# Border of the shared and routed expert stages: awaiting the output stores later, turning the first rows ahead of the register loads, and moving expert 0's last weight piece

## The reference

```python
h = rmsnorm(x, ln2_w)
t = h.reshape(-1, d)                       # T = 2048 tokens, d = 512
logits = t @ gate_w.T
probs = jax.nn.softmax(logits, axis=-1)
topv, topi = jax.lax.top_k(probs, K)       # K = 6 of E = 16 experts
topv = topv / jnp.sum(topv, axis=-1, keepdims=True)
cw = jnp.zeros((T, E), t.dtype).at[jnp.arange(T)[:, None], topi].add(topv)
g = jnp.einsum('td,eid->eti', t, eg_w)     # I = 352
u = jnp.einsum('td,eid->eti', t, eu_w)
hh = jax.nn.silu(g) * u
routed = jnp.einsum('eti,edi,te->td', hh, ed_w, cw)
shared = jax.nn.silu(t @ sg_w.T) * (t @ su_w.T) @ sd_w.T    # 704 = 2 x 352
out = x + (routed + shared).reshape(b, s, d)
```

## Time and profile before

| what | us |
|---|---|
| three runs: median | 2296.87 |
| three runs: lowest, highest | 2296.24, 2299.54 |
| the profiled execution's own time | 2293.54 |
| its span in the profile | 2291.5 |
| PE busy | 2163.1 (94% of the span) |
| DVE busy | 1180.4 (52%) |
| POOL busy | 989.1 (43%) |
| ACT busy | 690.7 (30%) |

### The profile page before, as it was taken

How to read it: one execution, slowest core, us unless ns; L and a number is a source line. 1 busy time by engine, 2 the same in 40 slices (tenths; PEclk the granted TensorE clock), 3 DMA queues, 4 the chain that set the end, 5 groups by cost and what they waited for, 6 DMA issues and landing times. The chain is left out here.

```text
span 2291.5 us, 40185 instructions
## 1 busy us (share of the span) xinstructions
PE 2163.1 (94%) x12066; PEld 1883.5 (82%) x12067; DVE 1180.4 (52%) x2533; ACT 690.7 (30%) x1609; POOL 989.1 (43%) x1043
## 2 busy tenths in 40 slices
PE   6879999999999999999994999979999999999997
PEld 4668888888888898888883767779999999998996
DVE  5736646564655646465665476533433333333342
ACT  5623334343333334333333211112222222222221
POOL 1225454553545454553546024424444444444443
PEclk9989999999999999999997999989999999999998
DMA  3113343343434344343336210076676676667443
GB/s 138 56 46 119 119 160 125 133 170 109 151 119 141 119 151 151 110 169 116 141 124 245 86 65 28 37 248 156 156 228 157 156 200 183 156 174 199 90 81 55
DMA packets 143417, 307.59 MB, mean 134 GB/s; under 512 B 17104, under 2 KB 17104, under 8 KB 141072
## 3 DMA queue, kind: packets, MB, share of 16 engines
q1 hardware_dynamic: 118128, 248.33, 30.9%
q0 software_dynamic: 24960, 58.21, 13.4%
q10 hardware_dynamic: 288, 0.53, 0.1%
HBM read 180.91 MB, written 126.09 MB: 134 GB/s over the span
## 5 line engine op out<-in xcount | busy, mean ns | idle before, releaser
L544 POOL TENSOR_TENSOR chunk_hi<-chunk_raw,zero 128x512 fp32r<-128x512 f32 x160 | 166.5, 1041 | 251.6 <-DMA chunk_raw<-in_whole 251.6
L1518 DVE TENSOR_TENSOR prod<-ps,silu 128x352 f32<-128x352 f32 x111 | 58.3, 525 | 313.4 <-PE ps L62 313.4
L546 POOL TENSOR_TENSOR chunk_raw<-chunk_raw,chunk_hi 128x512 fp32r<-128x512 f32 x160 | 206.8, 1293 | 12.5
L733 DVE TENSOR_TENSOR pT_lo<-ps,pT_hi 128x512 fp32r<-128x512 f32 (+3 forms) x256 | 119.8, 489 | 167.4 <-ACT pT_hi L679 167.4
L1368 POOL DMA_INDIRECT out<-y,sidx x111 | 176.5, 1590 | 54.2 <-issue 34.5
L1375 POOL TENSOR_TENSOR carry<-ident 128x1 f32<-128x1 f32 x218 | 41.2, 189 | 326.9 <-DVE gidx L1515 261.0
L707 DVE SCALAR_TENSOR_TENSOR HS<-ps,rinv,HS 128x512 f32<-128x512 f32 x260 | 176.7, 746 | 1.2 <-PE ps L62 1.2
L673 ACT ACTIVATE prob<-ps,negmax 128x512 f32<-128x512 f32 (+3 forms) x256 | 131.7, 528 | 112.1 <-DVE negmax L696 112.1
L60 PE MATMUL ps<-wv_or_qk_hi,hT_hi 128*128 128x256 f32 x512 | 145.7, 285 | 8.3 <-POOL wv_or_qk_lo L539 8.3
L60 PE MATMUL ps<-ring,xT_0hi 128*128 x448 | 150.5, 336 | 1.7 <-DMA ring<-split_weights 1.7
L60 PE MATMUL ps<-ring,hT_hi 128*128 x333 | 141.0, 423 | 7.9 <-issue 5.6
(11 more groups left out here) (293 smaller groups left out, 6216.4 us busy)
## 6 DMA issues: line engine op xcount, KB each, us to landing
ring<-split_weights SPq DMA_DIRECT2D x240, 272.0 KB, 6.8
chunk_raw<-in_whole SPq DMA_DIRECT2D x162, 256.0 KB, 2.7
split_weights<-chunk_hi SPq DMA_DIRECT2D x160, 256.0 KB, 2.4
split_weights<-chunk_raw SPq DMA_DIRECT2D x160, 256.0 KB, 2.6
xg<-in_wqk SPq DMA_DIRECT2D x17, 512.0 KB, 3.4
xg<-in_wv SPq DMA_DIRECT2D x9, 512.0 KB, 3.5
x<-in_x SPq DMA_DIRECT2D x4, 1024.0 KB, 5.6
x_spill<-x SPq DMA_DIRECT2D x4, 1024.0 KB, 3.9
```

The costliest lines, as they stand in the source:

```text
L544: nc.gpsimd.tensor_tensor(chunk_hi[k][:], chunk_raw[k][:], zero[:].to_broadcast([P, CH]), ALU.add).then_inc(chunk_high, 1)
L546: nc.gpsimd.tensor_tensor(chunk_raw[k][:].bitcast(F32R), chunk_raw[k][:], chunk_hi[k][:].bitcast(F32), ALU.subtract).then_inc(chunk_low, 1)
L733: nc.vector.tensor_tensor(pT[1][:, 0:i + 1, w], ps_t[k % 2][:, 0:(i + 1) * P].rearrange("p (j t) -> p j t", t=P), pT[0][:, 0:i + 1, w].bit ...
```

## The change

1. The pad rows of the output are set to zero in `normed_again`, from the `zeros` buffer that is there already, directly after the pad rows of `normed_rows`; the store from `silu`, DVE's memset of `silu` and SP's wait for it go away.
2. SP no longer waits for the output stores at the end of the shared stage. The semaphore `stored` is now made outside both stages. In the routed stage SP waits for it ahead of its first ring load, and GpSimd ahead of its first scatter (just before its loop).
3. SP issues expert 0's last piece (768 KB) ahead of the wait for the first of the last four sums, that is right behind the third batch's store.
4. In the routed stage PE turns the rows of unit 0, reads the registers and runs `gate_up` of unit 0 ahead of its wait for the two memsets; ACT and DVE no longer wait for them. The memset of `prod` covers only the 32 columns that the products don't write.

```diff
 # normed_again is called with pads(rows) + pads(out)

 # shared_expert, sync
             for b in range(NB - 1):
                 sp.wait_ge(dve_acc, ST * (STEPS - NB + b + 1))
                 sp.dma_start(out[b], HS[...]).then_inc(stored, 16)
+            sp.wait_ge(pe_u, NI * STEPS)
+            load_ring(1, slice(GU, EW))
             for i in range(ST):
                 t = TT - ST + i
                 sp.wait_ge(dve_acc, ST * (STEPS - 1) + i + 1)
-                if i == 0:
-                    sp.wait_ge(pe_u, NI * STEPS)
-                    load_ring(1, slice(GU, EW))
                 sp.dma_start(out[NB - 1][:, i, :], HS[:, t * D:(t + 1) * D]).then_inc(stored, 16)
-            sp.wait_ge(dve_z, 1)
-            for pad in pad_out:
-                sp.dma_start(pad, silu[:]).then_inc(stored, 16)
-            sp.wait_ge(stored, 16 * (NB - 1 + ST + len(pad_out)))
 # shared_expert, vector
-            nc.vector.memset(silu[:], 0.0).then_inc(dve_z, 1)
 # routed_experts
+    STORED = 16 * (NB - 1 + ST)
         def _(sp):
+            sp.wait_ge(stored, STORED)
             for e in range(1, E):
 # gpsimd
-            nc.gpsimd.memset(prod[:], 0.0).then_inc(pool_0, 1)
+            nc.gpsimd.memset(prod[:, I:NI * P], 0.0).then_inc(pool_0, 1)
             pool.wait_ge(pool_0, 2)
             pool.wait_ge(added, FIRST)
             for n in range(2):
                 step(n, n, scatters=False)
+            pool.wait_ge(stored, STORED)
             with pool.Fori(1, TURNS) as g:
 # tensor
+            transposed(1, 0)
+            first, its_expert = base(0), expert(0)
+            gate_up(first, its_expert, 0, 0)
             pe.wait_ge(pool_0, 2)
-            first, its_expert = base(0), expert(0)
-            transposed(1, 0)
-            gate_up(first, its_expert, 0, 0)
 # scalar
-            act.wait_ge(pool_0, 2)
             high_rows(0, 0)
 # vector
-            dve.wait_ge(pool_0, 2)
             dve.wait_ge(added, FIRST)
```

More of the change, by code:

```diff
@@ L919, in shared_expert @@
 def shared_expert(nc, sem, ps, ident, HS, hT, logits, token_of, weight_of, expert_of, base_of, ends_of,
-                  slab, warm, ring, split_w, out, pad_out, first_rows, rows, ld_rows, ld_ring, added, begin):
+                  slab, warm, ring, split_w, out, stored, first_rows, rows, ld_rows, ld_ring, added, begin):
     NBLK = T // S
@@ L983, in shared_expert @@
         pe_g, pe_u, act_s, dve_p, act_h, dve_h = (sem(k) for k in ("pe_g", "pe_u", "act_s", "dve_p", "act_h4", "dve_h4"))
-        pe_d, dve_acc, stored = sem("pe_d"), sem("dve_acc4"), sem("stored")
+        pe_d, dve_acc = sem("pe_d"), sem("dve_acc4")
         dve_r, dve_c, act_e, pe_r = sem("dve_r"), sem("dve_c"), sem("act_e"), sem("pe_r")
@@ L987, in shared_expert @@
         dve_unit, pe_unit = sem("dve_unit"), sem("pe_unit")
-        dve_z = sem("dve_z4")
         LOGITS, PICKED, PACKED = 1, 2, 3
@@ L1312, in routed_experts @@
 def routed_experts(nc, sem, ps, ident, token_of, weight_of, expert_of, base_of, ends_of, rows, ring, xg, ld_x, ld_ring,
-                   added, begin, split_w, out):
+                   added, begin, stored, split_w, out):
     NI = len(IT)
@@ L1561, in program @@
         begin = sb("begin", [P, 3])
-        ld_xg, ld_ring, added = [sem(f"ld_xg{q}") for q in range(2)], sem("ld_ring"), sem("added")
+        ld_xg, ld_ring, added, stored = [sem(f"ld_xg{q}") for q in range(2)], sem("ld_ring"), sem("added"), sem("stored")
         reserved = sb("slab", [P, WARM + 2 * GU], F32R)
@@ L1579, in program @@
             logits = stream.enter_context(nc.sbuf_tensor("logits", [P, TT, E], F32))
-            normed_again(nc, sem, ps, ident, neg_half, eps, HS, hT, logits, tiled(rows), pads(rows), ln2, gateT, spill,
+            normed_again(nc, sem, ps, ident, neg_half, eps, HS, hT, logits, tiled(rows), pads(rows) + pads(out), ln2, gateT, spill,
                          warm, split_w)
             shared_expert(nc, sem, ps, ident, HS, hT, logits, token_of, weight_of, expert_of, base_of, ends_of,
-                          slab, warm, ring, split_w, tiled(out), pads(out), xg, rows, ld_xg, ld_ring, added, begin)
+                          slab, warm, ring, split_w, tiled(out), stored, xg, rows, ld_xg, ld_ring, added, begin)
         routed_experts(nc, sem, ps, ident, token_of, weight_of, expert_of, base_of, ends_of, rows, ring, xg, ld_xg, ld_ring,
-                       added, begin, split_w, out)
+                       added, begin, stored, split_w, out)
 def kernel(**inputs):
```

## The result

| | before | after |
|---|---|---|
| median of 16 runs, us | 2296.73 | 2292.62 |
| lowest, highest | 2293.86, 2299.66 | 2289.36, 2296.26 |
| the profiled execution: its own time, its span | 2293.54, 2291.5 | 2295.15, 2293.2 |

The ratio is 0.9982 with a 95% interval of 0.9974 to 0.9990: the change saves 4.1 us, and 2.3 to 6.0 are possible. The forecast was 5.7 us. By the bound of 0.2% this is just inside "no change", though the interval excludes zero. One execution of e1 (3081.74 us) and one of before (5499.21 us) were in a slower state and are left out of the ratios.

What follows compares the result with a forecast made beforehand. PE was taken to bound the routed stage, so an earlier start ends it earlier: 2.15 (release) + 3.0 (transposes) + 0.5 (clock) = 5.7 us, from a median of 2296.87 to 2291.2 us; range 2287.6 to 2294.8.

Steps and rivals of the forecast that it cites:

- the bound of 0.2%: What a measurement of this kernel can tell from no change: about 0.2%, 4.6 us.
- The border's time: Between shared and routed stage, where PE waits 8.7 us: what PE starts earlier there, it ends earlier.
- The rival in which it doesn't hold the release: Stage border: GpSimd's drain doesn't hold, release at 1504.9, gain 7.4 us, 2289.5 us; chance 0.08.
- The rival of a border still held at 1508: Stage border: release still at about 1508, gain 3.0 to 4.5 us, 2293.2 us; chance 0.23.
- Parts 1 and 2: Shared stage's end: without SP's wait and pad store, release 2.15 us earlier; expert 0's piece issued 2 us earlier, 0.
- Part 3: Routed stage's head: transposes ahead of memsets and register loads, 3.0 us earlier, the loads covered.
- Part 4: Routed stage: SP's wait for stores ahead of ring loads, which begin 1.2 us earlier; cost 0.
- Part 5: `normed_again`: the 256 KB pad store delays DVE's group 2 by 0.7 us, but is covered; cost 0.
- the cover of 1.4 us: `normed_again`: slack left between DVE's four operations and ACT's copies that need them; without cover, 0.7 us cost.
- the shared stage began later than 1265: Sign in the profile after that the pad store's costing at 0 in `normed_again` was wrong.
- Part 6, the clock: First gate matmuls of the routed stage: half clock for 4.7 us instead of 5.8, gain 0.5 us.
- the routed stage from its first gate matmul to its end becomes longer: Sign in the profile after, over the routed stage, that the whole forecast is wrong.

Runs made afterwards that it cites:

- e1: The kernel before with only PE's order, ACT's and DVE's waits and the smaller memset changed; ratio to before 0.9986.
- e3: The changed kernel with the first two gathers issued at the head of the routed stage, not at the shared stage's end; ratio to before 0.9999.
- e6: The changed kernel with four more stores of zeros (1 MB) behind the output's pad store, ahead of group 0's store; ratio to before 0.9980.
- f3: The kernel before with only the loop's register loads moved ahead of PE's wait for gathered rows; ratio to before 1.0016, median 2299.56 us.
- e8: The kernel before, unchanged, run once more for a second profile; one run without a ratio, loop 753.0 us.
- e5: The changed kernel with the output's pad store issued at the end of `normed_again`, behind all stores of rows; ratio to before 0.9982.
- f1: The changed kernel with the loop's register loads moved ahead of PE's wait for gathered rows; ratio to before 0.9985, median 2293.75 us.
- e7: The changed kernel with the moves of both e4 and e5; ratio to before 0.9962.
- e4: The changed kernel with expert 0's last piece issued once PE has left its place, ahead of the third batch's store; ratio to before 0.9961.
- f2: e7 with the loop's register loads moved ahead of PE's wait as in f1; ratio to before 0.9980.

## Why the prediction was right

**What bounds it, and the drain.** The border's time did pass to the end, as far as the medians tell, and the drain is GpSimd's wait for its gathers: forecast to end at 1506.7, that is 2.4 us behind the last sum, measured at 2.3 to 2.5. e3 shows the cause itself. The rival in which it doesn't hold the release falls with it. The rival of a border still held at 1508 forecast 2293.2 us, and the median of 2292.62 is nearer to that than to the forecast's 2291.2; it is the release at 2.5 us behind the last sum, and not the time, that rules it out.

**Parts 1 and 2.** Forecast 2.15 us of release, measured 4.7 - 2.5 = 2.2. The piece's shift inside the backlog was costed at 0 and brought 0 as far as the drain's length shows; it was not run alone.

**Part 3.** Forecast 3.0 us, measured 3.1 in e1 alone. The register loads stayed hidden: the first gate matmul follows the transposes' start by 2.28 us. The hand-over after the release was 0.1 us, not 0.2.

**Part 4.** The ring loads waited 0.9 us for the stores and began 1.3 us earlier than before, forecast 1.2. The only wait for the ring that PE's list shows is 0.8 us at g1, the same as before.

**Part 5.** No cost was seen, as forecast, but the working was wrong. DVE's group 2 started 22.7 us after the stage's release against 22.6, not 0.7 later; and the cover of 1.4 us, worked out from one ACT instruction, is not confirmed: 2.4 us of delay in e6 changed no time that could be told. That the shared stage began later than 1265 had been named as the sign of this part being wrong. It did, by 2.3 us, but 0.8 of that stood there before the stage, and a stage as long (47.7 us) occurs in f3 without the store, so the sign doesn't tell this.

**Part 6, the clock.** This is the term that did not hold. The transposes ran at full clock (0.63 us for four, not 1.11), which brings the first gate matmul 0.6 us nearer to them (2.28 us for 2.86); the forecast had no such term. The gate matmuls ran at half for 5.2 us in after. From the first gate matmul to g1 it took 8.5 to 8.8 us with the change, and 8.75, 7.8 and 7.5 in the three profiles with the border of before (before, e8, f3). So the shorter stretch at half clock, on which I had put the gain, was not there: on average the stretch cost 0.7 us more. Together that is -0.1 us where 0.5 was forecast, and the first two profiles alone, with 0.8, hide it.

**The sum.** The four profiles of the changed border (after, e5, e6, f1) have g1 at 13.4 to 13.9, mean 13.7, and the three of the old one at 19.6, 18.5 and 18.0, mean 18.7: 5.0 us, which is 5.1 by the start of the transposes and -0.1 by the clock. The medians say 4.1 (after), 4.7 (e5), 4.4 (e6) and 5.8 (f1 against f3), each uncertain by about 2 us. The forecast of 5.7 is inside after's interval, and what it has too much is the clock's term. Counted from the mean of 18.7 and not from the first profile's 19.6, the border's gain and the measured one of e1 to e7 and after differ by -0.8 to 1.6 us, 0.5 on average, so no missing microsecond is shown. The loop does look longer in the profiles: 752.5 and 753.0 us in before against 753.7 to 758.1 in nine changed kernels with that loop. By the sign that the prediction had set (the routed stage from its first gate matmul to its end becomes longer) it would be wrong. But both profiled executions of before were faster than its median by 2 to 3 us, and five of eight changed ones were slower than theirs, so the profiles are not a fair sample; f1 and f3, with 2.6 us of difference in the loop, have medians that differ by more than the border; and no run here shows a way from the change into the loop. Whether the change touches the loop stays open.

**The chances.** 0.32 stood on within 0.2%, where it came out, and 0.65 on more: the likelier side was the wrong one. The bound of 4.6 us lay 1.1 us below the forecast, while the interval of the measurement is 3.7 us wide, so the chances were finer than any measurement could check. The median fell 0.5 us inside the bound, and with 2 us of uncertainty it is chance on which side of it a gain of 5 us is measured; without the clock's term the forecast would have been 5.2, outside it as well.

## What to carry to other kernels

Before a wait at a stage's end is taken away, look at what every engine's drain waits for: GpSimd's lasts here until its own gathers have landed, and it takes over the wait. A gather waits, beyond its own start of 1.7 to 1.9 us, for the backlog given to the plain queue before it, so a load that nobody needs yet belongs well ahead of it (e4, 15.7 us ahead: the drain ends 2.2 us sooner and the kernel is 4.8 us below after) and not just ahead of it (the drain as long as before). A single profile of a kernel whose executions differ by 3 us is read stretch by stretch from a common event; its span tells nothing of a change of 4 us. The common stretch needs more than one profile too: g1 stood at 19.6, 18.5 and 18.0 with one and the same border.

## What was not expected

- GpSimd's drain takes 0.3 us without outstanding gathers (e3) and 6.1 to 8.8 with them.
- 768 KB on q1 ahead of two gathers on q0 delay them by 2.2 us (the drain ends at +0.1 in e4 and at +2.3 in after). At the 338 to 389 GB/s of the stretches shown these bytes take 2.0 to 2.3 us (an estimate).
- After a pause of 3.3 us the four transposes still ran at full clock (0.63 us), and the matmuls 1.7 us later at half; after one of 1.5 us all ran at full clock in e4, but not in e7 and f2.
- A megabyte more ahead of a store for which DVE waits moved DVE's start by 2.4 us and the kernel by nothing that could be told.
- With three register loads moved ahead of PE's wait in the loop, the median unit took about 0.1 us longer.
